# Mixture layers: routing ahead of the shared expert, routers and down projections on strips

## The chip, the cores and the metric

One core of a Trainium2 chip. The metric is the time on the device of one launch, in microseconds. PE is TensorE, DVE VectorE, ACT ScalarE, POOL GpSimd, SP SyncE, which here only issues DMAs. Each engine works through its own list of instructions in order and meets the others through semaphores.

## The reference, cut to what matters

The program is two layers over x of 4096 tokens x 256, in float32. In each, x += 0.5 ffn(norm(x)), x += mixer(norm(x)), x += 0.5 ffn(norm(x)), with the same feed-forward both times. That of the first layer is a mixture of experts, and only it is changed:

```
scores = sigmoid(x @ router_w.T)                    # 32 experts
sc     = scores + e_bias
groups: 8 of 4 experts, score = sum of the two best; keep the 3 best groups
topk   = 4 best experts by sc in those; weight = its score, normalised, * 2.5
slots  : each expert takes the first 160 tokens that chose it
Y      = (silu(X Wg) * (X Wu)) Wd for the 160 tokens of each expert
out[token] += weight * Y ;  out += (silu(x Sg^T) * (x Su^T)) Sd^T    # shared expert
```

## The kernel before, in words

`moe()` (lines 476 to 1300) is called twice; its tiles are named ffn0a (layer a below, about 0 to 247 us) and ffn0b (layer b, about 509 to 744 us). Everything is written out by hand: each engine's list of work is a sequence of helper calls, at the end of that engine's function, and that sequence is the order of execution. No planner has a part in it.

*Norm phase.* The 4096 tokens are 8 blocks of 4 tiles of 128. For a block, DVE takes the moments (`moments`), POOL works out the reciprocal deviation and the shift (lines 718 to 728), ACT applies them (`apply`, line 977, four instructions), SP stores the rows to HBM for later gathering (`rows`), PE turns the eight 128x128 pieces (`turn`, L775) into one PSUM tile `ps_a`, and ACT copies them out (`turned`, L991), so that the next turn can begin. PE then makes the router's scores (`router`, L785): a turned tile of 128 tokens is stationary, the 32-column router weight moves, k innermost, 8 matmuls a block. After four blocks ACT makes the sigmoid of one half of the tokens (`scores`, Exp, Ln, Exp). PE's list starts with a few matmuls on constants (`warm`, L177).

*Shared expert.* For each of 6 of the blocks (two more come at the end of the layer), PE does two up projections `up(n, m)` (L809), ACT the silu `gate` (L996), DVE the product `hidden` (L1119), PE the two halves of the down projection (`down`, L819) into the one tile `ps_c`, ACT copies each half out (`keep`, L1013), and SP stores it. The up projections begin in the norm phase, between the turns and routers.

*Routing.* For each half DVE scores the groups, chooses groups and experts (`score_groups` L1125, `choose_groups`, `choose_experts` L1155), and weighs the scores (`weigh`). PE counts choices by triangular matmuls (`count`, L792 to L799); DVE splits the slot numbers, then for each of 4 groups of 8 experts makes planes for the slot numbering that PE does by matmuls (`number_slots`, L397), and from it the list of tokens (`dve_tokens`).

*Experts.* POOL gathers the rows of a group's tokens by indirect DMAs, ten a group (L436); group 2 waits until all up projections are done, since it uses their room. PE turns the rows (`turn_rows`, `spread`), does the expert's two projections (`expert_up`, L866) and its down projection (`expert_down`, L888), whose results land in pieces of 128 slots: 160 slots an expert, so five pieces to four experts. In `expert_down` a piece is put together from the parts that `rows_of` gives, of 32, 64 or 128 slots, each by one matmul. ACT weighs each piece while it copies it out (`keep_y`, L1038), POOL adds it to the sums in HBM by an indirect DMA (`add`, L737), 40 of them. The gathers of the last group stand between adds 6 to 15. Then the two late blocks' sums are loaded and the next layer's head norm follows.

Of the kernel before, what the change touches and what calls it, by code (L numbers as in the profile page):

```python
# [11 lines left out]
ALU = mybir.AluOpType  # L12
# [464 lines left out]
def moe(nc, name, x, con, w, table, sums, gathered, added, turn_no, spare, combine, head, arriving=None,  # L477
# [3 lines left out]
    with Scope(nc, name) as sc:  # L481
# [9 lines left out]
        ps_r = ps_d.rearrange("p (t e) -> p t e", e=E)  # L491
# [28 lines left out]
        esg, eh = sg[:, :, 0:CAP], h[:, 0, :, 0:CAP]  # L520
# [29 lines left out]
        shift_ready = sc.sem("shift_ready")  # L550
        raw_made = sc.sem("raw_made")
        exp_made = sc.sem("exp_made")
        plus_made = sc.sem("plus_made")
# [39 lines left out]

        def finished(e):

            return (CAP * (e + 1)) // P
# [21 lines left out]
        with nc.Block() as block:  # L618
            @block.sync
            def _(sp):  # L620
# [8 lines left out]
                def rows(b):  # L629
                    sp.wait_ge(ln.xn_ready, b + 1)  # L630
                    sp.dma_start(by_tile[:, b * BT:(b + 1) * BT, 0:D], ln.xn[:, b]).then_inc(ln.xn_stored[b % 2], 16)
# [15 lines left out]
                for dst, key in zip((wg, wu, wd), ("shared_gateT", "shared_upT", "shared_downT")):  # L647
                    sp.dma_start(dst[:], w[key].rearrange("(k p) n -> p k n", p=P)).then_inc(shared_landed, 16)
# [3 lines left out]
                rows(0)  # L652
                rows(1)
                start_sums(0)
                start_sums(1)
                rows(2)
                start_sums(2)
                rows(3)
                start_sums(3)
                if not ahead:  # L660
                    sp.wait_ge(zero_set, 1)
                    clear(sp, cleared[0], range(4), zero, zero_stored)
                rows(4)
                start_sums(4)
                rows(5)
                start_sums(5)
                if arriving:
                    arriving[4]()
                rows(6)
                start_sums(6)  # L670
                shared(0)
                rows(7)
                start_sums(7)
# [7 lines left out]
                shared(1)  # L681
                if not ahead:
                    clear(sp, cleared[1], range(4), zero, zero_stored)
                weights(0)
                weights(1)
                shared(2)
                if not ahead:
                    clear(sp, cleared[1], range(4, NB), zero, zero_stored)
                    clear(sp, other, LATE, zero, zero_stored)
                    sp.wait_ge(x_stored[1], 16 * (NB - 2))  # L690
                shared(3)
                if not ahead:
                    load(0)
                    load(1)
                for n in range(4, NF):
                    shared(n)
# [14 lines left out]
            def _(pool):  # L711
# [6 lines left out]
                for b in range(NB):  # L718
# [6 lines left out]
                    after(pool, ln.xn_ready, b - 1)  # L725
# [15 lines left out]

                pool.wait_ge(ln.transposed, NB)
# [24 lines left out]
            def _(pe):  # L767
                mm = nc.tensor.matmul

                def turn(b):  # L770
                    pe.wait_ge(ln.xn_ready, b + 1)
# [7 lines left out]
                def router(b):  # L779
                    r, part = divmod(b, RT // BT)  # L780
                    pe.wait_ge(ln.xT_ready, b + 1)
                    after(pe, exp_made, r)
                    for t in range(BT):
                        for k in range(KD):
                            ins = mm(ps_r[:, part * BT + t, :], xT_of(b)[:, k, t * P:(t + 1) * P], wr[:, k, :],  # L785
                                     start=k == 0, stop=k == KD - 1)
                    ins.then_inc(raw_made, 1)

# [82 lines left out]
                def rows_of(e):  # L871

                    at, end, parts = CAP * e, CAP * (e + 1), []
                    while at < end:
                        row = at % P
                        most = {0: P, QR: QR, 2 * QR: 2 * QR, 3 * QR: QR}[row]
                        n = min(most, end - at)
                        parts.append((at // P, row, at - CAP * e, n))
                        at += n
                    open_ended = [y for y in parts if y[0] >= finished(e)]  # L880
                    return open_ended + [y for y in parts if y[0] < finished(e)]

                def expert_down(e):
                    p, r, n = e % 2, e // LW % 2, e % LW
                    pe.wait_ge(eh_made, e + 1)
                    for piece, row, at, m in rows_of(e):
                        after(pe, piece_kept, piece - 1)
                        ins = mm(ps_b[row:row + m, 2 + piece % 2, 0:D], eh[:, p, at:at + m], we[:, r, n, 2, :],  # L888
                                 start=True, stop=True)
                        if row + m == P:  # L890
                            ins.then_inc(piece_made, 1)
# [9 lines left out]
                pe.wait_ge(shared_landed, 48)  # L901
                up(0, 0)
                turn(2)
                router(1)
                up(0, 1)
                turn(3)
                router(2)
                up(1, 0)
                router(3)
                turn(4)  # L910
                up(1, 1)
                turn(5)
                router(4)
                pe.wait_ge(halved, 1)
                down(0, 0)
                turn(6)
                router(5)
                down(0, 1)
# [3 lines left out]
                up(2, 0)  # L922
                pe.wait_ge(constants_set, 1)
                count(0)
                up(2, 1)
                down(1, 0)
                down(1, 1)
                up(3, 0)
                count(1)
                down(2, 0)  # L930
                up(3, 1)
                down(2, 1)
                up(4, 0)
                number_slots(0)
                down(3, 0)
                up(4, 1)
# [1923 lines left out]
```

## Time and profile before

| | |
|---|---|
| time, median of 3 runs | 1126.53 us (1124.96 to 1128.38) |
| profiled execution | 1118.18 us, span 1116.3 us |
| busy, share of the span | PE 980.2 us (88%), DVE 723.6 (65%), ACT 549.5 (49%), POOL 379.3 (34%) |

Busy time is that of instructions, without their waits; a share is an average over stages. A row of the timeline gives the start, the duration of a run of like instructions, engine, line, operation, output and inputs, the shape, how many; in brackets how long the engine was idle before it, and what ended that. Matmuls overlap their neighbours, so the distance from one start to the next says more than a duration. The granted clock is 1.00 at 2.4 GHz and 0.50 at 1.2 GHz.

### The profile page before, as it was taken

The page shows a single profiled execution, that of the slowest core. Times are in us where ns is not written, and L with a number is a line of the kernel's source. Part 1 is how long each engine was busy: PE and PEld are TensorE (multiplying, and loading weights), DVE is VectorE, ACT ScalarE, POOL GpSimd, SP SyncE. Part 2 cuts the span into 40 slices and gives each one's busy share as a digit, 9 for nine tenths or more (in the row PEclk, how much of TensorE's full clock was granted, in tenths as well). Part 3 has the DMA queues.
Part 4 walks back from the last instruction along what each step waited for, and adds up shares of the span by engine and source line. Part 5 has one row for each costly group of instructions (what it writes and reads, how often), then busy time and mean ns, then how long its engine had stood idle before and what let it go on. Part 6 is the DMA issues. An engine that isn't in the chain of part 4 may idle for free. (4 is left out here: it accounts for less than half of the span.)

```text
span 1116.3 us, 17327 instructions
## 1 busy us (share of the span) xinstructions
PE 980.2 (88%) x5222; PEld 601.4 (54%) x5240; DVE 723.6 (65%) x2533; ACT 549.5 (49%) x1066; POOL 379.3 (34%) x452
## 2 busy tenths in 40 slices
PE   6999799979999899998999898946778799995886
PEld 4756566645565466665756665533334456552343
DVE  4588333147885476766598433158888799974886
ACT  6621233325665654547622333226657655544784
POOL 3106768810000232323006787711111256531110
PEclk9999799989999699999999999976889999996998
DMA  9859888854440902004245878766420000000012
GB/s 323 323 179 318 157 220 212 155 166 151 151 151 0 344 6 94 38 38 144 95 150 130 183 195 193 142 193 208 151 75 1 1 0 1 1 0 1 20 56 76
DMA packets 79656, 140.73 MB, mean 126 GB/s; under 512 B 16304, under 2 KB 47392, under 8 KB 77472
## 3 DMA queue, kind: packets, MB, share of 16 engines
q1 hardware_dynamic: 64224, 117.57, 30.6%
q0 software_dynamic: 15360, 22.29, 13.0%
q8 instruction: 33, 0.54, 0.2%
q14 instruction: 39, 0.32, 0.1%
HBM read 82.17 MB, written 58.72 MB: 126 GB/s over the span
## 5 line engine op out<-in xcount | busy, mean ns | idle before, releaser
L737 POOL DMA_INDIRECT ffn_sums<-ffn0a_xT,ffn0a_into x40 | 62.6, 1566 | 19.5 <-issue 8.5
L737 POOL DMA_INDIRECT ffn_sums<-ffn0b_xT,ffn0b_into x40 | 62.5, 1563 | 14.5 <-issue 9.5
L2717 PE MATMUL main_ps_k<-mixing_first_xk,mixing_wk 128*128 128x512 f32 (+1 forms) x96 | 46.7, 610 | 4.2 <-POOL main_opened_mark L1962 4.2
L1768 POOL TENSOR_TENSOR attn_attend_state_m<-attn_attend_state,attn_attend_heads 128x512 f32<-128x512 f32 x15 | 19.1, 1273 | 87.1 <-DVE attn_attend_state L1811 81.6
L1193 DVE TENSOR_TENSOR ffn0a_h<-ffn0a_sg,ffn0a_ps_b 128x160 f32<-128x160 f32 x32 | 10.3, 321 | 55.4 <-ACT ffn0a_sg L1028 55.3
L1193 DVE TENSOR_TENSOR ffn0b_h<-ffn0b_sg,ffn0b_ps_b 128x160 f32<-128x160 f32 x32 | 10.3, 321 | 53.8 <-ACT ffn0b_sg L1028 53.7
L2722 PE MATMUL attn_ps_r<-mixing_first_xr,mixing_wr 128*128 128x512 f32 (+1 forms) x96 | 45.1, 592 | 0.0
L2732 PE MATMUL attn_ps_y<-mixing_wv,attn_out 128*128 128x256 f32 (+1 forms) x192 | 43.0, 379 | 1.2 <-ACT attn_yn L2674 1.2
L866 PE MATMUL ffn0a_ps_b<-ffn0a_early,main_x 128*128 128x160 f32 x256 | 43.2, 314 | 0.7 <-DMA main_x<-w_experts 0.7
L888 PE MATMUL ffn0a_ps_b<-main_x,ffn0a_h 128*32 128x256 f32 (+2 forms) x144 | 43.5, 403 | 0.0
L888 PE MATMUL ffn0b_ps_b<-main_x,ffn0b_h 128*32 128x256 f32 (+2 forms) x144 | 43.5, 403 | 0.0
L2291 PE MATMUL main_ps_k<-dense_first_xb,main_w 128*128 128x512 bf16 x112 | 39.2, 423 | 4.7 <-issue 1.9
L1790 DVE COPY_PREDICATED main_spare<-attn_attend_causal,attn_attend_ps_a 128x1024 f32<-128x1024 int32 x32 | 40.0, 1302 | 4.5 <-issue 2.9
L866 PE MATMUL ffn0b_ps_b<-ffn0b_early,main_x 128*128 128x160 f32 x256 | 41.3, 305 | 1.5 <-DMA main_x<-w_experts 1.2
L866 PEld LDWEIGHTS ffn0a_ps_b<-ffn0a_early,main_x 128*128 128x128 f32 x256 | 38.4, 198 | 6.2 <-issue 3.8
L2732 PEld LDWEIGHTS attn_ps_y<-mixing_wv,attn_out 128*128 128x128 f32 (+1 forms) x192 | 36.3, 190 | 9.5 <-issue 3.4
L866 PEld LDWEIGHTS ffn0b_ps_b<-ffn0b_early,main_x 128*128 128x128 f32 x256 | 36.6, 190 | 7.1 <-issue 3.5
L1351 DVE TENSOR_TENSOR main_spare<-main_spare 128x1024 f32<-128x1024 f32 x28 | 34.1, 1219 | 6.8 <-POOL main_opened_mark L1962 5.9
L2593 DVE TENSOR_TENSOR_SCAN attn_st<-mixing_keep,mixing_first_carry,attn_kr 128x512 f32<-128x512 f32 (+1 forms) x24 | 31.8, 1326 | 8.6 <-ACT attn_kr L2667 8.6
L256 POOL TENSOR_TENSOR attn_head_ln_ve<-attn_head_ln_moments,attn_head_ln_eps 128x4 f32<-128x4 f32 x8 | 2.1, 266 | 103.5 <-DVE attn_head_ln_moments L232 103.5
L1811 DVE SCALAR_TENSOR_TENSOR attn_attend_state<-attn_attend_state,attn_decay,attn_attend_ps_s 128x256 f32<-128x256 f32 x32 | 14.0, 477 | 33.2 <-PE attn_attend_ps_s L1909 33.2
L1924 PE MATMUL attn_attend_ps_w<-attn_attend_wo,attn_attend_cent 128*128 128x256 f32 x128 | 31.9, 394 | 2.1 <-DVE attn_attend_cent L1805 2.1
(498 smaller groups left out, 2665.1 us busy)
## 6 DMA issues: line engine op xcount, KB each, us to landing
main_spare<-ffn_sums SPq DMA_DIRECT2D x28, 1024.0 KB, 5.5
main_x<-w_experts SPq DMA_DIRECT2D x16, 1536.0 KB, 7.0
ffn_sums<-main_lent SPq DMA_DIRECT2D x36, 512.0 KB, 6.1
ffn_sums<-main_x SPq DMA_DIRECT2D x28, 512.0 KB, 3.8
ffn_rows<-ffn0a_early SPq DMA_DIRECT2D x8, 512.0 KB, 9.3
main_spare<-ffn_sums SPq DMA_DIRECT2D x8, 512.0 KB, 4.7
ffn_rows<-ffn0b_early SPq DMA_DIRECT2D x8, 512.0 KB, 2.9
x_out<-main_x SPq DMA_DIRECT2D x8, 512.0 KB, 2.9
```

Source lines behind the costliest of these rows:

```text
L737: g.indirect_dma_start(out=sums[:, :], out_offset=IndirectOffsetOnAxis(ap=into[:, at, j:j + 1], axis=0), in_=ys[:, n % NY, :], in_offset=N ...
L866: ins = mm(ps_b[:, p, j * CAP:(j + 1) * CAP], we[:, r, n, j, k * F:(k + 1) * F], xgT[:, k, e // ME % 2, e % ME].rearrange("p a b -> p (a b)"),
L888: ins = mm(ps_b[row:row + m, 2 + piece % 2, 0:D], eh[:, p, at:at + m], we[:, r, n, 2, :], start=True, stop=True)
L1193: v.tensor_tensor(eh[:, p, :], esg[:, p, :], ps_b[:, p, CAP:2 * CAP], ALU.mult).then_inc(eh_made, 1)
L1351: v.tensor_tensor(parts[:, half, 0:2], parts[:, half, 0:2], parts[:, half, 2:4], ALU.add)\
L1790: vec.copy_predicated(att[:, p, s].rearrange("p (r n) i -> p r n i", n=2), causal[:].unsqueeze(1).unsqueeze(1).to_broadcast([P, 4, 2, P]), ...
L1924: ins = mm(ps_w[:, s, :], cent[:, 1 - p, k, s, :], wo[:, k, :], start=k == 0, stop=k == KD - 1)
L2291: ins = mm(ps[:], wt[:, k, m * P:(m + 1) * P], xb[:, p, k, :], start=k == 0, stop=k == KD - 1)
L2593: v.tensor_tensor_scan(st[0:rows, m % 2], keep[0:rows, m:m + 1].to_broadcast([rows, BN]), kr[0:rows, m % 2], carry[0:rows, p, m:m + 1], AL ...
L2717: ins = mm(ps_k[0:rows, m % 2], wk[:, k, at:at + rows], xk[:, p, k, :], start=k == 0, stop=k == KD - 1)
L2722: ins = mm(ps_r[0:rows, m % 2], wr[:, k, at:at + rows], xr[:, p, k, :], start=k == 0, stop=k == KD - 1)
L2732: ins = mm(ps_y[:, t, :], out[0:rows, p, m, t * P:(t + 1) * P], wv[0:rows, m, :], start=m == 0, stop=m == NMH - 1)
```

## The change

1. Norm. `apply` of the even blocks goes to DVE, of the odd ones stays on ACT; a semaphore for each, and `normed(b)` names the one to wait for.
2. Router. The router weight is stationary (128x32), the turned tile moves (128 columns), and the four tiles of a block go to the four 32-partition strips of a PSUM bank. The sigmoid runs on these turned scores; PE turns four 128x128 pieces back (`turn_back`) and ACT copies them out (`keep_scores`).
3. Order. On PE all turns and routers come ahead of the first up projection; on ACT the applies, copies and sigmoids ahead of the first gate; on DVE the choice of the first half ahead of the first hidden. SP loads the shared weights after x, stores the router's weights and (layer a) loads the first expert weights ahead of the first shared block.
4. `weigh` goes from DVE to POOL.
5. `expert_down` does a piece when its last expert is there: one matmul of 128 slots where the piece is all of one expert, else four strips of 32. The hidden tile of an expert has three buffers instead of two.

```diff
+        ps_raw = (ps_d, ps_c)
+        esg = sg[:, :, 0:CAP]
+        eh = [h[:, at, m, 0:CAP] for at, m in ((0, 0), (0, 1), (1, 0))]
+        def normed(b):
+            return (xn_by_act if b % 2 else xn_by_dve), b // 2 + 1
...
 # SP
-                for dst, key in zip((wg, wu, wd), ...): sp.dma_start(...)     # now after the loads of x
...
+                for b in range(NB):
+                    rows(b)
+                    start_sums(b)
...
+                weights(0)
+                weights(1)
+                if not ahead:
+                    sp.wait_ge(x_stored[1], 16 * (NB - 2))
+                    load(0)
+                    load(1)
+                shared(0)
...
 # POOL
+                def weigh(r):
+                    pool.wait_ge(score_made, r + 1)
+                    pool.wait_ge(taken_ready, r + 1)
+                    g.tensor_tensor(score[:, r], taken[:, r * RT:(r + 1) * RT, :], score[:, r], ALU.mult)\
+                        .then_inc(weight_ready, 1)
+                for r in range(NR):
+                    weigh(r)
                 pool.wait_ge(ln.transposed, NB)
...
 # PE
-                    after(pe, exp_made, r)
-                    for t in range(BT):
-                        for k in range(KD):
-                            ins = mm(ps_r[:, part * BT + t, :], xT_of(b)[:, k, t * P:(t + 1) * P], wr[:, k, :],
+                    for k in range(KD):
+                        for t in range(BT):
+                            ins = mm(ps_raw[r][t * E:(t + 1) * E, part * P:(part + 1) * P], wr[:, k, :],
+                                     xT_of(b)[:, k, t * P:(t + 1) * P], start=k == 0, stop=k == KD - 1,
+                def turn_back(r):
+                    pe.wait_ge(sigmoid_made, r + 1)
+                    for part in range(BT):
+                        ins = nc.tensor.transpose(ps_b[:, 2 + r, part * P:(part + 1) * P],
+                                                  sg[:, r, part * P:(part + 1) * P], con[:, C_IDENT:C_IDENT + P])
+                    ins.then_inc(back_made, 1)
+                def parts_of(n):
+                    parts = []
+                    for q in range(P // QR):
+                        at = P * n + QR * q
+                        parts.append((at // CAP, QR * q, at % CAP, QR))
+                    if parts[0][0] == parts[-1][0]:
+                        return [(parts[0][0], 0, parts[0][2], P)]
+                    return parts
                 def expert_down(e):
                     pe.wait_ge(eh_made, e + 1)
+                    for n in range(finished(e - 1) if e else 0, finished(e)):
+                        after(pe, piece_kept, n - 1)
+                        for of, row, at, m in parts_of(n):
+                            ins = mm(ps_b[row:row + m, 2 + n % 2, 0:D], eh[of % 3][:, at:at + m],
+                                     we[:, of // LW % 2, of % LW, 2, :], start=True, stop=True, ...)
+                        ins.then_inc(piece_made, 1)
...
 # PE's list: turn(0) turn(1) router(0) turn(2) router(1) turn(3) router(2) router(3) turn(4) turn(5) router(4)
+                turn_back(0)
 #            turn(6) router(5) turn(7) router(6) router(7)
+                up(0, 0)
+                turn_back(1)
+                pe.wait_ge(score_made, NR)
+                up(0, 1)
+                count(0)
+                up(1, 0)
+                down(0, 0)
+                down(0, 1)
+                count(1)
+                for n in range(1, NF):
+                    up(n, 1)
+                    if n + 1 < NF:
+                        up(n + 1, 0)
+                    down(n, 0)
+                    down(n, 1)
+                    if n < 4:
+                        number_slots(n - 1)
                 number_slots(3)
...
 # ACT
+                def sigmoids(r): Exp, Ln, Exp on sg[:, r] from ps_raw[r]
+                def keep_scores(r): Copy of ps_b[:, 2 + r] to score[:, r]
 # ACT's list: apply(1) turned(0) turned(1) apply(3) turned(2) turned(3) apply(5) sigmoids(0) turned(4) keep_scores(0)
 #             turned(5) apply(7) turned(6) turned(7) sigmoids(1) (wd halved) keep_scores(1) gate(0, 0) gate(0, 1)
+                for n in range(NF):
+                    if n:
+                        gate(n, 1)
+                    if n + 1 < NF:
+                        gate(n + 1, 0)
+                    keep(n, 0)
+                    keep(n, 1)
...
 # DVE
+                def apply(b): four tensor_scalar (x - mean) * rstd
-                    after(dve, piece_made, finished(e - 2) if e > 1 else 0)
+                    after(dve, piece_made, -(-CAP * (e - 2) // P) if e > 2 else 0)
+                moments(0)
+                for b in range(1, NB):
+                    moments(b)
+                    if b % 2:
+                        apply(b - 1)
 # DVE's list goes on: score_groups(0) choose_groups(0) choose_experts(0) hidden(0, 0) score_groups(1) hidden(0, 1)
 #   choose_groups(1) count_first_half choose_experts(1) with hidden(1, 0) inside, split_slots(0) hidden(1, 1)
 #   split_slots(1) planes(0, row) hidden(2, 0) planes(0, halves) planes(1, row) tokens(0) hidden(2, 1) ...
```

## Rows read from the trace of the kernel before

**Rows 1.** Grouped lines of POOL, whole span (busy us, mean ns; idle before, by releaser).

```profile
L737 POOL DMA_INDIRECT ffn_sums<-ffn0a_xT,ffn0a_into x40 | 62.6, 1566 | 19.5 <-issue 8.5 <-ACT ffn0a_xT L1038 6.9 <-DMA ffn_sums<-ffn0a_xT,ffn0a_into 4.1
...
L737 POOL DMA_INDIRECT ffn_sums<-ffn0b_xT,ffn0b_into x40 | 62.5, 1563 | 14.5 <-issue 9.5 <-DMA ffn_sums<-ffn0b_xT,ffn0b_into 3.8 <-ACT ffn0b_xT L1038 1.2
...
L436 POOL DMA_INDIRECT ffn0b_xT<-ffn_rows,ffn0b_token x20 | 20.8, 1040 | 6.1 <-issue 4.6 <-ACT ffn0b_xT L1038 1.5
```

**Rows 2.** Timeline of layer b, anchors (start us, us).

```profile
558.70 0.69 DVE L1125 TENSOR_TENSOR ffn0b_masked<-ffn0b_score,ffn0b_bias 128x512 f32<-128x512 f32 x1 [4.27 <-ACT ffn0b_score L987]
...
574.44 0.43 DVE L1155 TENSOR_SCALAR ffn0b_taken<-ffn0b_marked 128x512 bf16<-128x512 f32 x1
...
611.23 1.97 PE L819 MATMUL ffn0b_ps_c<-ffn0b_shared_down,ffn0b_h 128*128 128x256 f32 x8 [0.78 <-ACT main_x L1013]
...
614.57 1.31 PE L397 MATMUL ffn0b_ps_d<-ffn0b_val_a,main_spare 128*128 128x80 f16 x32 [1.38 <-DVE ffn0b_val_a L389]
...
615.71 1.07 PE L839 MATMUL ffn0b_ps_a<-main_con,ffn0b_early 128*128 128x128 f32 x8
...
620.27 1.90 PE L866 MATMUL ffn0b_ps_b<-ffn0b_early,main_x 128*128 128x160 f32 x12 [0.34 <-ACT ffn0b_early L1021]
...
632.86 1.62 POOL L737 DMA_INDIRECT ffn_sums<-ffn0b_xT,ffn0b_into  x1 [0.30 <-issue]
```

**Rows 3.** Timeline of PE in layer b, its pieces from start to start.

```profile
515.16 1.09 PE L775 MATMUL ffn0b_ps_a<-main_con,ffn0b_early 128*128 128x128 f32 x8 [0.72 <-ACT ffn0b_early L977]
...
526.82 1.96 PE L809 MATMUL ffn0b_ps_b<-ffn0b_xT,ffn0b_shared_gate 128*128 128x512 f32 x4
...
530.34 1.04 PE L775 MATMUL ffn0b_ps_a<-main_con,ffn0b_early 128*128 128x128 f32 x8
...
574.92 0.39 PE L792 MATMUL ffn0b_ps_a<-ffn0b_taken,ffn0b_before 128*128 128x512 bf16 x1
...
577.01 1.97 PE L819 MATMUL ffn0b_ps_c<-ffn0b_shared_down,ffn0b_h 128*128 128x256 f32 x8
...
578.82 1.02 PE L809 MATMUL ffn0b_ps_b<-ffn0b_xT,ffn0b_shared_gate 128*128 128x512 f32 x2
```

**Rows 4.** Timeline of PE in the last layer, matmuls on 32-column strips.

```profile
747.74 1.08 PE L2025 MATMUL main_ps_k<-dense_ln_xT,main_router 128*32 128x128 f32 x16 [1.17 <-ACT dense_ln_xT L2000]
...
1067.08 0.64 PE L2025 MATMUL main_ps_k<-dense_ln_xT,main_router 128*32 128x128 f32 x16
...
1067.65 0.38 PE L2300 MATMUL ffn1b_ps_c<-ffn1b_gate_t,main_pick 16*128 16x512 bf16 x1
```

**Rows 5.** Grouped lines of ACT (500 to 620 us) and of POOL (whole span).

```profile
L977 ACT ACTIVATE ffn0b_early<-main_x,ffn0b_shift,ffn0b_ln_rstd 128x256 f32<-128x256 f32 x32 | 16.3, 591 | 2.7 <-POOL ffn0b_shift L728 2.7
...
L991 ACT ACTIVATE ffn0b_xT<-ffn0b_ps_a 128x1024 f32<-128x1024 f32 x6 | 6.1, 1014 | 0.6 <-PE ffn0b_ps_a L775 0.5
...
L996 ACT ACT_TABLE_LOAD x3 | 3.8, 1283 | 0.1
...
L1768 POOL TENSOR_TENSOR attn_attend_state_m<-attn_attend_state,attn_attend_heads 128x512 f32<-128x512 f32 x15 | 19.1, 1273 | 87.1 <-DVE attn_attend_state L1811 81.6 <-PE attn_attend_ps_a L1886 5.5
```

**Rows 6.** Windows of PE: length, busy (instructions), granted clock, DMA share, GB/s.

```profile
53.00:55.00 2.00, 2.00 (x16) 0.80 1.04 384
...
55.00:57.00 2.00, 2.00 (x4) 0.50 1.02 401
...
746.00:748.00 2.00, 0.83 (x11) 0.50 0.13 18
```

**Rows 7.** Timeline of PE in layer a, down matmuls four experts apart.

```profile
199.77 1.25 PE L888 MATMUL ffn0a_ps_b<-main_x,ffn0a_h 128*32 128x256 f32 x4
...
209.57 0.40 PE L888 MATMUL ffn0a_ps_b<-main_x,ffn0a_h 128*32 128x256 f32 x1
```

**Rows 8.** Timeline of layer a, its first turn and its first add.

```profile
12.94 1.09 PE L775 MATMUL ffn0a_ps_a<-main_con,ffn0a_early 128*128 128x128 f32 x8 [1.74 <-ACT ffn0a_early L977]
...
132.46 1.62 POOL L737 DMA_INDIRECT ffn_sums<-ffn0a_xT,ffn0a_into  x1 [0.95 <-ACT ffn0a_xT L1038]
```

More of the change, by code:

```diff
@@ L651, in _ @@
                         arriving[2](n)
[L652 to L673, printed above, removed]
+                for dst, key in zip((wg, wu, wd), ("shared_gateT", "shared_upT", "shared_downT")):
+                    sp.dma_start(dst[:], w[key].rearrange("(k p) n -> p k n", p=P)).then_inc(shared_landed, 16)
+                for b in range(NB):
+                    rows(b)
+                    start_sums(b)
+                    if b == 3 and not ahead:
+                        sp.wait_ge(zero_set, 1)
+                        clear(sp, cleared[0], range(4), zero, zero_stored)
+                    if b == 5 and arriving:
+                        arriving[4]()
                 if ahead:
@@ L689, in _ @@
                     clear(sp, other, LATE, zero, zero_stored)
[L690 to L695, printed above, removed]
+                for n in range(2, NF):
                     shared(n)
@@ L1139, in mark_best @@
                     link(ins)
+                    if between:
+                        hidden(*between)
                     link(v.memset(top[:, :, n:8], LOW_MARK))
@@ L1242, in _ @@
                 choose_groups(0)
-                hidden(1, 1)
-                choose_experts(0)
-                score_groups(1)
-                hidden(2, 0)
-                choose_groups(1)
-                hidden(2, 1)
-                count_first_half()
-                choose_experts(1)
-                split_slots(0)
-                weigh(0)
-                hidden(3, 0)
+                choose_experts(0)
+                hidden(0, 0)
+                score_groups(1)
+                hidden(0, 1)
+                choose_groups(1)
+                count_first_half()
+                choose_experts(1, between=(1, 0))
+                split_slots(0)
+                hidden(1, 1)
                 split_slots(1)
@@ L1256, in _ @@
                 index.dve_planes(0, row)
-                weigh(1)
+                hidden(2, 0)
                 index.dve_planes(0, tile_a)
-                hidden(3, 1)
                 index.dve_planes(0, tile_b)
```

165 lines of the change are left out of this document (53 added, 112 removed).

## The prediction

> **What bounds the kernel now.** I read the busy shares first: PE is busy most of the span, POOL a third of it; those are averages, and the change touches only the two mixture layers (called a and b here, about 0 to 247 and 509 to 744 us). Next the grouped lines of POOL: in each layer the 40 scatter-adds stand 62.5 us busy beside 14.5 (b) and 19.5 (a) of idle, of which 9.5 and 8.5 are POOL's own issue: an add at POOL's own pace is 1.56 and up to 0.3, 1.86 [rows 1]. With the ten gathers of the last group between them ((20.8 + 6.1) / 20 = 1.34 each) they fill the end of the layer: POOL is the bound there, and little of its idle is another engine's doing (b: DMA 3.8, ACT 1.2; a: ACT 6.9, DMA 4.1). So a layer's length is the start of its first add plus that loop. The timeline says what sets this start. In b PE ends its shared expert at 611.23 plus 1.1, the last slot numbering starts at 614.57, the first expert matmul at 620.27 and the first add at 632.86 [rows 2]. Two lines race to that add: PE's in-order list up to the first expert, and POOL's gathers of group 2, which wait for the shared expert's last up projection, because they reuse its buffers, and then take 10 x 1.34 = 13 us.
>
> **The change, part by part.** It takes the shared expert's work out of the gaps of the norm phase and puts it behind the routers; so the question is whether the norm phase gets shorter by as much as PE's later list gets longer.
>
> *Norm phase.* Per pair of blocks ACT has one apply (16.3 / 8 = 2.04) and two copies of turned blocks (1.01 each) [rows 5]; the other apply goes to DVE, which has slack. The turned tile has one buffer, so the second turn waits for the first copy and the second copy for that turn: 1.09 at full clock [rows 3] and 0.1 of hops. A pair takes 2.04 + 1.01 + 1.2 + 1.01 = 5.25, four take 21. The three sigmoid passes and the copy-back over 128x512 are half-size against 1.01: 2.0, with hops 2.5; the last routers trail by 1.4. From the first turn, 515.16 [rows 3], the last router ends at 515.2 + 21 + 2.5 + 1.4 = 540.1. The strip routers cost little: 16 strip matmuls of the same shape take 0.57 from start to start at full clock, and a row of 1.08 in a stage at half [rows 4].
>
> *Clock.* This is where I choose. PE keeps 2.4 GHz through the present norm phase because projections fill its gaps. Where the present kernel leaves turns and old routers by themselves, the granted clock falls to 0.80 and then 0.50 within 4 us, and the next projection's first four matmuls, at full clock 1.8, don't end within that window of 2 us [rows 6]. In a later stage turns and strip routers with gaps stay at 0.50 [rows 6]. After the change PE does only these, and about half the time, for some 25 us. I take it to fall to 1.2 GHz. Then a turn is 2.0 instead of 1.1 (a pair 6.15, four 24.6) and the last routers trail by 2.2: the last router ends at 544.5.
>
> The Trainium skill, "TensorE: Matmul & The Clock Gate", Part 4, says that transposes do not count as busy for the gate as matmuls do; by that rule the clock falls here as in rows 6, and the sum is the one with 1.2 GHz. The trace agrees (0.80, 0.50).
>
> *From the last router to the second half's choice.* One projection (526.82 to 530.34 = 3.5; at half clock about 1.5 more) [rows 3], the turn back 0.5, the copy 0.6, ACT's table load 1.28 [rows 5], the gate 0.6, and DVE's hidden 0.7 stand one behind another, since the new order puts hidden(0,0) ahead of the second half's scoring: 540.1 + 7.2 = 547.3, at half clock 544.5 + 8.7 = 553.2. Then DVE does score_groups, two hiddens, choose_groups, the first half's count and choose_experts, as it does now between 558.70 and 574.44 + 0.43: 16.2 [rows 2]. The choice is there at 563.5 (569.4), where it is 574.9 now: 11 (5.5) earlier, and the first token list and POOL's first gathers with it.
>
> *PE behind it.* count(1) waits for this choice, and PE's order is fixed. Three projections and two downs lie ahead of it, 10.5 + 3.6 and the first count 2.1 and the turn back 0.5, in a stretch of 563.5 - 540.1 = 23.4: PE idles some 6 us, which would be another reason for the clock to fall. Behind it stand count(1) 2.1, nine projections x 3.5 = 31.6, ten downs x 1.81 = 18.1 [rows 3], four slot numberings x 1.14 (614.57 to 615.7) = 4.6 [rows 2]: 56.4. Each second down of a block waits for ACT's copy of the first: five times 0.78 [rows 2] = 3.9. Where a hidden stands behind index work on DVE (a row of planes and two halves), PE waits too: I allow 3.7, between nothing and five times the 1.38 that the last slot numbering waits now [rows 2]. Sum 64.0: the last numbering ends at 627.5 (633.4). From there to the first expert now 4.56 (615.71 to 620.27): 632.1 (638.0), against 620.27. The first add follows by one expert's up, gate, hidden, one piece and its copy, 4.6 as I estimate it (1.3 for eight up matmuls at the pace of the first twelve, 1.90 [rows 2], 0.6 for the gate, 0.4 for hidden, 1.1 for two pieces, 0.6 for the copy, hops 0.6), with 2 to either side; today's 12.6 can't be its size, since the gathers set it. So the first add moves from 632.86 to 636.7 (642.6): 3.8 or 9.7 later. Now it is the gathers that hold it 12.6 behind the first expert; then the gathers, behind a last projection that ends at 627.5 - 1.1 - 3.6 - 0.8 = 622, are through by 622 + 0.5 + 13.4 = 636 and tie with PE.
>
> *Layer a.* The same order, from the first turn at 12.94 [rows 8] by the same distance, 632.1 - 515.2 = 116.9: first expert at 129.8 (135.8), add at 134.4 (140.4), against 132.46: 1.9 or 7.9 later.
>
> *Expert loop.* Four experts take PE 199.77 to 209.57 = 9.80 [rows 7]; the ups at the pace above take 4 x 1.27, so nine down matmuls take 4.7, 0.53 each. New: three sets of four strips and two full matmuls. If strips overlap as in rows 4, a set of 256 columns is twice 0.57 / 2 = 0.57, so 3 x 0.57 + 2 x 0.53 = 2.8: PE gains 1.9 per four experts, 15 a layer. POOL needs 5 x 1.86 + 1.25 x 1.34 = 11.0 for the same pieces, so this stays hidden; only waits on ACT's copies can shrink. I take 4 of the 6.9 in layer a, 0 in b; the ends are 0 and 6.9 + 1.2. No row shows strips of 256 columns with a changing weight, so the cost of a set lies between 0.57 and 4 x 0.53 = 2.1.
>
> The Trainium skill, "TensorEngine Tiling (Array Packing)", Key Properties, says that a change of the tiling mode drains TensorE; this speaks against a loop that goes from strips to full matmuls with every expert. By it a set would cost more than 0.57; rows 4 show no such drain (the next instruction of another shape starts 0.57 after 16 strips).
>
> *The rest.* weigh goes to POOL: 1.27 each by the nearest row of that shape [rows 5], twice, while POOL has nothing but norm steps and waits for tokens some 15 us away; if it were late, 2.5. SP's queue gets the shared weights later and the expert weights earlier; the first user of either stands behind the last router. Two table loads fewer on ACT (1.28 each) lie in the norm phase of which I have already counted what is left. Those I set at 0 with ends of -2.5 and +2.5.
>
> **Sum.** With the clock low: b +9.7, a +7.9 - 4 = +3.9: +13.6. The profiled execution (1118.2) then gives 1131.8; it lies 8.3 below the median 1126.53, to which I add the same: 1140.
>
> **The rivals.**
> A, the clock stays high in the norm phase. For it: the four filling matmuls between the first turns remain. Against it rows 6. Then +3.8 + 1.9 - 4 = +1.7: 1128, no change.
> B, faster: PE does not wait for the second choice, and its list sets the first expert. Without that idle and the waits of 3.7 and 3.9: 540.1 + 12 x 3.5 + 12 x 1.81 + 2 x 2.1 + 4.6 + 0.5 = 613.1, first expert 617.7; the last projection ends 4.8 before 613.1 and the gathers 13.9 later, so the add comes at about 622, 10.6 earlier in b, and by the same distance at 120 in a, 12.5 earlier and 4 more in the loop. Half of the 27 gives 1113, all of it 1100. It decides if the choice comes before 540.1 + 16.7 = 557. For it: DVE loses its 4.27 wait for the second score in the old place. Against it: 16.2 of chained DVE work behind the first hidden is in the order itself.
> C, slower: strips one behind another. Then 14 x 0.53 = 7.4 instead of 4.7 per four experts, PE at 12.5 against POOL's 11.0: 1.5 x 8 x 2 = +24, on the forecast 1164. It decides from a set of about 1.6 us. Against it rows 4.
> D, the norm phase isn't shortened because something else paces it (in a the arrival of the blocks): another +3 to +5, inside the forecast's own range.
>
> **How the numbers follow.** Forecast (D included) 0.5; A 0.2; B 0.23; C 0.07. Forecast's own range 1132 to 1150, from the allowance of 3.7 (0 to 6.9 in each layer), the 4.6 (by 2), and the 4 (0 to 8). The range of 8 in 10 reaches through A to the weaker half of B: 1112 to 1150. About 0.3% (3.4 us, so 1123 to 1130) is what a measurement of this kernel can tell from no change. Faster: B and a little of A, 0.27. Same: most of A and the forecast's lower edge, 0.17. Slower: 0.56.
>
> **What would show it.** Granted clock near 0.50 between the second turn and the first projection; the second choice near 569 and first expert near 638 counted from a start of 509 in b; an idle stretch of PE before its second count; the add loop no shorter than now in b; PE's matmuls per four experts near 7.9 us. The prediction is wrong if the first add comes before 632.86 counted from the same start, or if the adds begin to run faster than 1.86 apart.

## The result, and the profile after

1141.59 us (1137.32 to 1144.88) against 1126.10 (1124.96 to 1128.38): a ratio of 1.0142, interval 1.0119 to 1.0166, so 13 to 19 us slower. 1140 was forecast. The page of the changed kernel shows how the work shrank while the time grew: PE has 20 us less to do than before, in a span 23 us longer (the profiled execution of before lies 8 us below its median, that of the changed kernel at its own; of the 23, 6.5 lie in layer a up to its last add, 11.8 in layer b, 1.6 between the two and 3.6 behind them, where nothing was changed). Every distance below is from one profiled execution of a kernel, and such an execution can lie several us from the median of its kernel.

```profile
span 1139.7 us, 17686 instructions
PE 960.4 (84%) x5416; PEld 581.8 (51%) x5416; DVE 732.1 (64%) x2561; ACT 526.4 (46%) x1030; POOL 388.2 (34%) x456
```

The timeline of layer b, which now starts 8.0 us later (first turn 523.17, in place of 515.16 [rows 3]), PE and DVE in the order of time, then POOL; the bracket is the engine's idle time before the row:

```profile
523.17 1.04 PE L779 MATMUL ffn0b_ps_a<-main_con,ffn0b_early 128*128 128x128 f32 x8
...
537.82 1.94 PE L779 MATMUL ffn0b_ps_a<-main_con,ffn0b_early 128*128 128x128 f32 x8 [3.10 <-ACT ffn0b_xT L995]
...
542.58 0.69 DVE L1125 TENSOR_TENSOR ffn0b_masked<-ffn0b_score,ffn0b_bias 128x512 f32<-128x512 f32 x1 [6.72 <-ACT ffn0b_score L990]
...
549.53 1.98 PE L820 MATMUL ffn0b_ps_b<-ffn0b_xT,ffn0b_shared_gate 128*128 128x512 f32 x4
...
572.44 0.61 PE L803 MATMUL ffn0b_ps_a<-ffn0b_taken,ffn0b_before 128*128 128x512 bf16 x1 [4.54 <-DVE ffn0b_taken L1156]
...
573.27 3.41 PE L810 MATMUL ffn0b_ps_a<-ffn0b_taken,ffn0b_ones 128*128 128x480 bf16 x15
...
590.74 1.84 PE L397 MATMUL ffn0b_ps_d<-ffn0b_val_a,main_spare 128*128 128x80 f16 x32 [2.09 <-DVE ffn0b_val_a L389]
592.38 3.11 PE L820 MATMUL ffn0b_ps_b<-ffn0b_xT,ffn0b_shared_gate 128*128 128x512 f32 x4
...
639.64 1.31 PE L397 MATMUL ffn0b_ps_d<-ffn0b_val_a,main_spare 128*128 128x80 f16 x32
...
645.30 2.44 PE L877 MATMUL ffn0b_ps_b<-ffn0b_early,main_x 128*128 128x160 f32 x16 [0.34 <-ACT ffn0b_early L1025]
...
634.44 1.00 POOL L436 DMA_INDIRECT ffn0b_xT<-ffn_rows,ffn0b_token  x1 [11.93 <-PE ffn0b_ps_b L820]
...
650.72 1.62 POOL L732 DMA_INDIRECT ffn_sums<-ffn0b_xT,ffn0b_into  x1 [3.55 <-ACT ffn0b_xT L1042]
```

Read it as a relay. The last router is done at 549.5, 26.4 after the first turn; that part is shorter than before. PE then waits 4.54 us for the second choice, comes out of the wait at half clock (15 matmuls of the count take 3.41, in place of 1.80 in the kernel before, whose row stands below), and works down its list to 640.8. POOL, which had its first gathers early, stands idle 11.93 us until the last projection has freed the room for group 2, and 3.55 more until ACT hands it the first piece. Before, the gathers ran without a break into the first add; now PE's list leads and POOL waits. From first turn to first add layer b takes 650.72 - 523.17 = 127.55 us, where it took 632.86 - 515.16 = 117.70 [rows 2, 3]: 9.85 more. Layer a: 142.00 - 12.89 = 129.1 against 119.5 [rows 8]: 9.6 more. The count in the kernel before, and the first add of layer a after:

```profile
575.36 1.80 PE L799 MATMUL ffn0b_ps_a<-ffn0b_taken,ffn0b_ones 128*128 128x480 bf16 x15
```

```profile
142.00 1.63 POOL L732 DMA_INDIRECT ffn_sums<-ffn0a_xT,ffn0a_into  x1 [3.56 <-ACT ffn0a_xT L1042]
```

The windows of PE (length, busy, granted clock, DMA share, GB/s) say when the clock falls:

```profile
526.00:530.00 4.00, 3.02 (x48) 1.00 0.61 207
530.00:534.00 4.00, 2.59 (x43) 1.00 0.83 295
534.00:538.00 4.00, 0.90 (x8) 0.83 0.83 280
538.00:542.00 4.00, 3.81 (x28) 0.50 0.27 87
570.00:574.00 4.00, 1.56 (x4) 0.60 0.00 0
574.00:578.00 4.00, 4.00 (x16) 0.55 0.76 197
586.00:590.00 4.00, 1.97 (x8) 1.00 0.00 0
590.00:594.00 4.00, 3.26 (x34) 0.66 0.32 131
```

Three falls in this execution, each at a wait: for the turn behind the first sigmoid (3.10 us), for the second choice (4.54), and for the first slot numbering, where DVE's planes come late (2.09; a wait of 0.78 for ACT stands shortly before). Through the 8 us of turns and strip routers before 534, which follow the constant matmuls of `warm`, with waits up to 1.2 us, the clock stayed at 1.00. That the same waits do not always end in a fall is shown by e4_old_down below.

The loop of adds, as POOL's grouped lines show it (to be set beside [rows 1]):

```profile
L732 POOL DMA_INDIRECT ffn_sums<-ffn0b_xT,ffn0b_into x40 | 62.5, 1563 | 19.7 <-issue 10.4 <-ACT ffn0b_xT L1042 5.2 <-DMA ffn_sums<-ffn0b_xT,ffn0b_into 4.1
L732 POOL DMA_INDIRECT ffn_sums<-ffn0a_xT,ffn0a_into x40 | 62.5, 1563 | 19.1 <-issue 9.2 <-ACT ffn0a_xT L1042 6.5 <-DMA ffn_sums<-ffn0a_xT,ffn0a_into 3.3
```

Of ACT's 5.2 (b) and 6.5 (a), 3.55 stand ahead of the first add, outside the loop. From first to last add: a 90.4 us (93.5 before), b 91.0 (89.0). So PE's quicker down projection is hardly seen here, though the grouped lines of PE in layer b show it plainly: 224 instructions in 27.1 us, where 144 took 43.5. What PE gains it waits for, in part, on the experts' weights (7.7 us in four waits; 1.2 before). The new order of SP's loads is not the reason: e3 and e6 below, which have the new down projection and the old order of loads, wait 8.6 and 9.5 us for them.

```profile
L898 PE MATMUL ffn0b_ps_b<-main_x,ffn0b_h 128*32 128x256 f32 (+1 forms) x224 | 27.1, 416 | 0.6 <-DVE ffn0b_h L1188 0.6
```

```profile
L888 PE MATMUL ffn0b_ps_b<-main_x,ffn0b_h 128*32 128x256 f32 (+2 forms) x144 | 43.5, 403 | 0.0
```

```profile
PE ffn0b_ps_b L877 <- DMA main_x<-w_experts: 7.7, 4, 3.9
```

And a set of four strips of 256 columns, in layer a's timeline, takes 0.57 from start to start; to the set four experts on (four experts, with one piece of index work in between) it is 7.96:

```profile
199.99 0.64 PE L898 MATMUL ffn0a_ps_b<-main_x,ffn0a_h 128*32 128x256 f32 x8
200.56 0.67 PE L863 MATMUL ffn0a_ps_c<-ffn0a_by_piece,main_con 128*128 128x80 f32 x4
...
207.95 0.64 PE L898 MATMUL ffn0a_ps_b<-main_x,ffn0a_h 128*32 128x256 f32 x8
```

### The profile page after: what moved, and what is told of

It reads as the page before. It is cut to its first block and busy times, and to the rows that moved or that the text cites. A ratio compares the mean times of both kernels' runs of the same rounds, so it can differ in the third digit from the quotient of the medians.

```text
span 1139.7 us, 17686 instructions
## 1 busy us (share of the span) xinstructions
PE 960.4 (84%) x5416; PEld 581.8 (51%) x5416; DVE 732.1 (64%) x2561; ACT 526.4 (46%) x1030; POOL 388.2 (34%) x456
## 5 line engine op out<-in xcount | busy, mean ns | idle before, releaser
L2284 PE MATMUL main_ps_k<-dense_first_xb,main_w 128*128 128x512 bf16 x128 | 45.1, 438 | 0.5
L830 PE MATMUL ffn0b_ps_c<-ffn0b_shared_down,ffn0b_h 128*128 128x256 f32 x112 | 28.6, 401 | 10.3 <-DVE ffn0b_h L1119 5.6
L830 PE MATMUL ffn0a_ps_c<-ffn0a_shared_down,ffn0a_h 128*128 128x256 f32 x112 | 28.3, 397 | 8.6 <-ACT main_x L1017 4.7
L1000 ACT ACTIVATE ffn0a_sg<-ffn0a_ps_b 128x512 f32<-128x512 f32 x14 | 8.4, 597 | 54.8 <-PE ffn0a_ps_b L820 54.8
```

The lines of the kernel that those rows point to most:

```text
L830: ins = mm(ps[:, i, :], h[:, n % 2, m, t * P:(t + 1) * P], wd[:, m, :], start=m == 0, stop=m == 1)
L2284: ins = mm(ps[:], wt[:, k, m * P:(m + 1) * P], xb[:, p, k, :], start=k == 0, stop=k == KD - 1)
```

## The experiments

The theory: the first expert comes late because PE's fixed list puts nine projections behind a count that waits for the second choice, with the clock down on top; POOL covers the rest. The rivals: the clock alone; one of the new parts; DVE's index work or the gathers. All times of the table but the last column's are counted from the layer's first turn, from one profiled execution each; a / b are the layers. The second count is given by its second matmul, which starts 0.2 us (at half clock 0.4) behind the end of the wait for the choice. Some profiled executions lie far from their kernel's median: before 8 us below, e7_both 8 below, e4_old_down 5 below, e3_strips_only 6 above. So differences of 2 or 3 us in this table are within its spread; the ratios are from all fast runs.

| kernel | ratio to before (95%) | last router starts | second count | first expert | first add | adds, first to last |
|---|---|---|---|---|---|---|
| before | 1 | 39.9 / 39.3 | 60.6 / 60.0 | 112.6 / 105.1 | 119.5 / 117.7 | 93.5 / 89.0 |
| changed | 1.0142 (1.0119 to 1.0166) | 27.3 / 25.8 | 51.0 / 49.7 | 123.7 / 122.1 | 129.1 / 127.6 | 90.4 / 91.0 |
| e1_clock | 1.0077 (1.0046 to 1.0108) | 25.0 / 25.0 | 49.1 / 49.1 | 117.5 / 117.5 | 123.0 / 123.0 | 93.3 / 92.6 |
| e2_up11 | 1.0080 (1.0027 to 1.0132) | 27.3 / 25.8 | 50.9 / 49.5 | 119.6 / 114.2 | 125.0 / 119.6 | 92.0 / 92.4 |
| e7_both | 1.0076 (1.0043 to 1.0108) | 25.0 / 25.0 | 49.1 / 49.1 | 118.7 / 113.7 | 124.2 / 119.1 | 89.7 / 91.2 |
| e4_old_down | 1.0197 (1.0155 to 1.0239) | 27.4 / 25.0 | 51.1 / 49.4 | 121.0 / 119.1 | 126.5 / 124.5 | 93.6 / 93.2 |
| e3_strips_only | 0.9976 (0.9953 to 1.0000) | 39.9 / 39.3 | 62.3 / 60.0 | 115.5 / 104.9 | 121.8 / 118.2 | 93.6 / 90.4 |
| e9_half_norm | 1.0003 (0.9974 to 1.0032) | 40.3 / 40.3 | 62.6 / 61.0 | 115.1 / 105.9 | 121.7 / 117.9 | 93.8 / 89.3 |
| e13_strip_router | 0.9985 (0.9961 to 1.0010) | 41.0 / 36.9 | 62.2 / 57.9 | 111.9 / 104.6 | 121.4 / 115.9 | 95.1 / 88.3 |
| e6_old_order | 0.9940 (0.9911 to 0.9970) | 36.0 / 36.0 | 57.2 / 57.0 | 108.2 / 102.0 | 115.4 / 114.1 | 95.0 / 90.5 |
| e10_earlier_scores | 0.9920 (0.9888 to 0.9952) | 35.0 / 35.0 | 58.0 / 57.0 | 110.1 / 101.9 | 116.8 / 113.9 | 91.7 / 88.3 |

**e1_clock: the clock held up.** Constant matmuls in PE's three waits.

```diff
                 turn(4)
+                warm(nc, con, ps_b[:, 0], 3)
                 turn(5)
                 router(4)
                 turn_back(0)
+                warm(nc, con, ps_b[:, 0], 1)
...
                 down(0, 1)
+                warm(nc, con, ps_d[:], 4)
                 count(1)
...
+                    if n == 1:
+                        warm(nc, con, ps_d[:], 2)
                     if n < 4:
                         number_slots(n - 1)
```

> The changed kernel with constant matmuls put into the three stretches in which PE waits (four of them in the norm phase before the sixth and seventh turn, four ahead of the second count, two ahead of the first slot numbering); order and all other work as changed. If the low clock carries most of the loss (the forecast against its rival A): granted clock 1.00 from the first turn to the first expert, last router, second choice and first expert 3 to 5 us earlier after the first turn, first add 6 to 8 us earlier in each layer, 1127 to 1131 us. If the order alone carries it: under 3 us off 1141.6.

The time fell from 1141.59 to 1133.55 (the ratio to before from 1.0142 to 1.0077), between the two expectations. The windows of that run that answer to those above (first turn at 517.68):

```profile
525.00:529.00 4.00, 2.23 (x44) 1.00 0.63 216
529.00:533.00 4.00, 4.00 (x30) 1.00 0.83 284
533.00:537.00 4.00, 3.25 (x31) 1.00 0.49 162
564.00:568.00 4.00, 2.50 (x12) 1.00 0.00 0
```

Its timeline behind the second choice shows the count back at 1.80, and the first expert:

```profile
566.54 0.39 PE L803 MATMUL ffn0b_ps_a<-ffn0b_taken,ffn0b_before 128*128 128x512 bf16 x1 [1.50 <-DVE ffn0b_taken L1161]
...
566.98 1.80 PE L810 MATMUL ffn0b_ps_a<-ffn0b_taken,ffn0b_ones 128*128 128x480 bf16 x15
...
635.22 2.03 PE L877 MATMUL ffn0b_ps_b<-ffn0b_early,main_x 128*128 128x160 f32 x13 [0.34 <-ACT ffn0b_early L1030]
```

So the clock carries about half the loss: the first expert comes 6.1 (a) and 4.6 us (b) sooner. But the front gives little of it. The second count starts only 2.0 and 0.6 sooner, because DVE, from the first half's score on, works some 30 us without a break to the second choice (0.4 us of waits in the changed kernel's layer b, none shown here), and that first score comes only 1.8 (a) and 0.4 us (b) sooner. In b the score is 536.68 - 517.68 = 19.0 after the first turn, where it was 542.58 - 523.17 = 19.4:

```profile
536.68 0.69 DVE L1130 TENSOR_TENSOR ffn0b_masked<-ffn0b_score,ffn0b_bias 128x512 f32<-128x512 f32 x1 [4.66 <-ACT ffn0b_score L995]
```

The rest, 4.1 and 4.0, lies behind the count. Both layers end their adds less far ahead of the changed kernel (3.2 and 3.0), since the loop got 2.9 and 1.6 longer.

**e2_up11: one projection ahead of the count.**

```diff
                 down(0, 1)
+                up(1, 1)
                 count(1)
                 for n in range(1, NF):
-                    up(n, 1)
+                    if n > 1:
+                        up(n, 1)
```

> The changed kernel with one projection, up(1,1), moved from behind the second count to ahead of it, into PE's idle stretch of 4.5 us. If PE's list behind the second count sets the first expert (forecast): the count isn't later, the list behind it is 3.5 shorter and its clock stays up (2.5), first add 5 to 6 us earlier in each layer, 1129 to 1132 us. If DVE's index work or POOL's gathers set the first add instead: no gain, 1139 to 1143.

1132.67, just above the 1129 to 1132 expected: the first add comes 4.1 (a) and 8.0 us (b) sooner, 6 a layer as expected in the mean. PE's list behind the second count is what sets it; POOL's gathers and DVE's index work allowed all of it in b. Only 3.5 of the 8.0 are the projection itself. PE's wait for the second choice shrank to 1.12 us, the count behind it took 1.80 again, and the first slot numbering 1.31, so most of the rest is clock, and the run does not separate the two. In a PE waited 3.42 us, in place of 0.78, for a copy of ACT that waited for a store (see e7):

```profile
113.19 0.60 ACT L1019 ACTIVATE main_x<-ffn0a_ps_c 128x512 f32<-128x512 f32 x1 [3.77 <-DMA ffn_sums<-main_x]
```

That this gain and that of e1 can't be added is shown by the next run.

**e7_both:** the matmuls of e1 in the norm phase and ahead of the first slot numbering, and the projection of e2 in the place of those ahead of the count.

> The changed kernel with constant matmuls in the norm phase and ahead of the first slot numbering, and up(1,1) moved ahead of the second count. The clock (8 us of the loss by the first run) and the idle stretch (9 by the second) share the slow second count, so the two don't add up: first add 3 us earlier than with the constant matmuls alone, 1126 to 1130 us. If they were independent: 1122 to 1125.

1130.43, a ratio of 1.0076, no better than either; what makes up the rest of the loss was not found, and the profiled execution can't tell, since it is the fastest of six (1122.09). In b the first add is 3.8 us sooner than in e1, as expected; in a it is 1.2 later. There something else ends last. ACT's copy of a shared block waits for the store of an earlier one, and PE's down projection behind it:

```profile
112.26 0.60 ACT L1023 ACTIVATE main_x<-ffn0a_ps_c 128x512 f32<-128x512 f32 x1 [4.46 <-DMA ffn_sums<-main_x]
```

```profile
113.00 3.65 PE L830 MATMUL ffn0a_ps_c<-ffn0a_shared_down,ffn0a_h 128*128 128x256 f32 x8 [4.11 <-ACT main_x L1023]
```

The DMA engines are 0.98 to 1.04 busy from 70 to 110 us in that layer, which alone has the clearing of the sums in its queue. So in a, as I read it, the shared expert, pushed together behind the routers, runs into the stores; no run moved the clearing away to show it.

**e3_strips_only** and **e4_old_down: the new down projection given and taken away.** e3 is the kernel before with the new `expert_down`, `parts_of` and three hidden buffers; e4 the changed kernel with the old ones:

```diff
-        esg = sg[:, :, 0:CAP]
-        eh = [h[:, at, m, 0:CAP] for at, m in ((0, 0), (0, 1), (1, 0))]
+        esg, eh = sg[:, :, 0:CAP], h[:, 0, :, 0:CAP]
...
-                        for of, row, at, m in parts_of(n):
...
+                    for piece, row, at, m in rows_of(e):
...
```

> The kernel before with the new down projection of the experts alone (strips, three hidden buffers). If POOL bounds the expert loop: PE's matmuls for four experts fall from 9.8 to about 7.7 us and the time stays, 1121 to 1127 us, the add loop at most 4 us shorter in layer a. If the loop is PE's: 10 us or more faster. If strips cost more than their overlap gives: slower.

> The changed kernel with the old down projection of the experts (two hidden buffers, parts of 32, 64 and 128 slots). If POOL bounds the loop: first add unchanged, 1141 to 1147 us, the most of it in layer a's adds. If the new down projection has part in the loss: faster than 1139.

e3: 1122.70, 0 to 5 us faster by its interval, although PE does the same experts in 16 us less per layer. e4: 1143.64. Its interval overlaps with that of the changed kernel, and its loop of adds is 2 to 3 us longer. Both say the same: POOL hides nearly all of it, and it has no part in the loss.

One thing in e4 was not expected: its first add comes 2.6 (a) and 3.1 us (b) sooner, though up to the first expert its work and order are those of the changed kernel. The clock did it. In b PE waits the same 3.10 us behind the first sigmoid and 2.10 ahead of the first slot numbering, and the clock stays at 1.00 behind both; in a it stays up behind the second of them:

```profile
536.28 1.06 PE L778 MATMUL ffn0b_ps_a<-main_con,ffn0b_early 128*128 128x128 f32 x8 [3.10 <-ACT ffn0b_xT L996]
...
586.45 1.31 PE L397 MATMUL ffn0b_ps_d<-ffn0b_val_a,main_spare 128*128 128x80 f16 x32 [2.10 <-DVE ffn0b_val_a L389]
```

```profile
535.00:539.00 4.00, 2.23 (x28) 1.00 0.63 212
586.00:590.00 4.00, 3.55 (x38) 1.00 0.30 119
```

So with the same list a wait of that length can end in a fall or not. It is also a second measure of the clock: without the fall at the first slot numbering, and with a shorter one at the count, the first expert comes 2.6 (a) and 3.0 us (b) sooner.

**e9_half_norm** and **e13_strip_router: two more parts alone,** in the order of before: four of the eight applies on DVE; the strip router with the sigmoid on turned scores, in one PSUM bank and turned back into it.

```diff
-                apply(0)
                 apply(1)
                 turned(0)
-                apply(2)
...
+                moments(0)
+                for b in range(1, 6):
+                    moments(b)
+                    if b % 2:
+                        apply(b - 1)
```

```diff
+                    for k in range(KD):
+                        for t in range(BT):
+                            ins = mm(ps_d[t * E:(t + 1) * E, part * P:(part + 1) * P], wr[:, k, :], ...)
...
                 turn(5)
+                turn_back(0)
                 router(4)
...
                 up(2, 0)
+                turn_back(1)
```

> The kernel before with half of the norms applied on DVE, in the order of before otherwise. If ACT paced the norm phase: second count 1 to 4 us earlier after the first turn, and 0 to 5 us faster, 1120 to 1126. If DVE or PE did: same as before, or up to 3 us slower, since the applies delay DVE's first hiddens.

> The kernel before with the strip router and the sigmoid on turned scores alone (one PSUM bank, turned back into the same bank). If the shorter router is what makes the version with the old order faster (second count 3.4 us earlier there): second count 57 to 59 after the first turn, first add 1 to 4 us earlier, 1117 to 1124 us. If it needs the half norms beside it (ACT paces): as before, 1122 to 1128.

Neither moves the time by more than its interval (1.0003, 0.9985). With the router alone the second count comes 2.1 us sooner in b, and 1.6 later in a; but e3, whose front is that of before, has it 1.7 later in a too, so in a that much is spread. With half of the norms alone it comes 2.0 (a) and 1.0 us (b) later. Together, in e6, they bring it 3.4 and 3.0 sooner.

**e6_old_order: all parts, the old order.** The two diffs above and the new down projection together in the kernel before, projections in the norm phase as they were; `weigh` stays on DVE.

> All parts of the change but the order: the kernel before, with its interleaving of projections into the norm phase, with half of the norms on DVE, strip routers with the sigmoid on turned scores (in one PSUM bank, turned back into the same bank), and the new down projection; weigh stays on DVE. If the order is what costs, and the parts are free or better: second count at 54 to 59 after the first turn (60 now), first add 3 to 8 us earlier than before in each layer, 1108 to 1122 us. If one of the parts costs: at or above 1126.

1117.79, 0.994 (0.9911 to 0.9970): faster than before, and 2% faster than the changed kernel, which differs from it by the order (SP's too), by `weigh`, and by the banks that the router writes. No run moves these apart, but `weigh` can be ruled out by the changed kernel's trace: POOL does the second one in 1.16 us, right behind the choice, and then has nothing to do for 21.41 us until its first gather:

```profile
572.53 1.16 POOL L741 TENSOR_TENSOR ffn0b_score<-ffn0b_taken,ffn0b_score 128x512 f32<-128x512 bf16 x1 [15.38 <-DVE ffn0b_taken L1156]
...
595.10 1.13 POOL L436 DMA_INDIRECT ffn0b_early<-ffn_rows,ffn0b_token  x1 [21.41 <-DVE ffn0b_token L421]
```

The rows of e6's layer b (first turn at 511.62) show POOL going from the last gather into the first add with its own 0.30 only, while PE had its first expert 12 us ahead of that add:

```profile
613.62 1.08 PE L884 MATMUL ffn0b_ps_b<-ffn0b_early,main_x 128*128 128x160 f32 x6 [0.34 <-ACT ffn0b_early L1045]
```

```profile
624.37 1.00 POOL L436 DMA_INDIRECT ffn0b_xT<-ffn_rows,ffn0b_token  x1 [0.30 <-issue]
625.67 1.62 POOL L747 DMA_INDIRECT ffn_sums<-ffn0b_xT,ffn0b_into  x1 [0.30 <-issue]
```

**e10_earlier_scores: the same with the scores drawn forward** (PE's part of the edit; ACT's sigmoid and DVE's scoring of the first half move ahead likewise).

```diff
                 router(2)
-                up(1, 0)
                 router(3)
                 turn(4)
-                up(1, 1)
+                up(1, 0)
+                turn_back(0)
                 turn(5)
-                turn_back(0)
                 router(4)
+                up(1, 1)
...
-                up(2, 0)
                 turn_back(1)
+                up(2, 0)
```

> The version with the old order and all parts, with the scores drawn forward: the fourth router ahead of up(1,0), the first half's sigmoid ahead of gate(1,0), the second turn back ahead of up(2,0). If the choice, and through it POOL's first gather, sets the first add there (first gather 74 and first add 114 to 115 after the first turn): second count 2 to 4 us earlier, first add as much, 1110 to 1117 us. If PE's list is the bound again: no gain, 1115 to 1121.

1112.71, 0.992 (0.9888 to 0.9952), the fastest kernel here; its interval overlaps with that of e6, so it is not shown to be faster than that. The time lies in the range expected, but the mechanism expected did not show: the second count is where it was (58.0 / 57.0) and the first add is no earlier (1.4 later in a, 0.1 sooner in b). The loop of adds is 2 to 3 us shorter instead; why was not tried.

## Why the prediction was right, and where it was not

**The path.** Right in each link: the last router earlier, PE idle ahead of the second count (6 us said, 4.5 measured), the first expert later, POOL waiting for PE where before POOL's own gathers had set the first add. The sum at half clock had the first add 9.7 (b) and 7.9 us (a) later; it came 9.85 and 9.6 later. That the total came within 2 us of 1140 is in part luck. From profile to profile the two layers grew by 18.3 (first add 19.4, loops -1.1), where the sum had 13.6, and the whole by 23.4; by the medians it is 15.5. The sum went from a profiled execution that was 8 us fast to a median, and errors of some us cancel there.

**PE behind the second choice.** 64.0 us to the end of the last slot numbering was the sum; with the clock up it is 111.9 + 1.1 - 48.9 = 64.1 (e1, b, from the end of the wait), and in the changed kernel 640.8 - 572.4 = 68.4. The sum was right for 2.4 GHz, which was assumed for this stretch; its step that failed is that assumption, by 4.3 us. The second choice, which starts this stretch, came 49.3 behind the first turn, 564.4 on the old start: where the sum with the clock high had it (563.5), not the one that was chosen (569.4).

**The clock: size right by luck, place and reason wrong.** 5.9 us a layer were put on the norm phase (last router 29.3 after the first turn instead of 24.9, and a slow first projection). Measured, the last router ends at 26.4 (b) and 27.9 (a), 0.8 and 2.3 behind e1; the first projection runs at full clock (549.53, 1.98). The second count is 0.6 and 2.0 late. The other 4 us lie behind the count, in two falls that the sum did not price. The sum holds in total, 6.1 and 4.6 by e1, only because these two were left out as the first was overpriced. The reason given was that turns and strips do not keep the clock up; the windows show 8 us of them at 1.00, and the fall behind the wait of 3.1 us, and e4's layer b goes through the whole norm phase, that wait included, at 1.00. By the Trainium skill, "TensorE: Matmul & The Clock Gate", Part 4, transposes do not count as busy in the way that matmuls do; this trace has turns mixed with strip matmuls, and through these 8 us the clock did not fall.

**The first add behind the first expert.** 4.6 estimated, 5.4 measured, within its 2.

**The tie of the gathers.** 636 against 636.7 was the forecast; the gathers end 3.6 us ahead of the first piece, so PE leads clearly.

**The loop.** Layer a was to gain 4 and gained 3.1; layer b was set at 0 and lost 2.0. With the first add earlier the loops grow to 92 to 93 us in both layers in e1 and e2, but not in e7 (89.7 and 91.2). What ends last in them was not settled: POOL's waits there spread over its own issue, DMA and ACT.

**The down projection.** 0.57 a set, 7.9 for four experts, 15 us a layer off PE, hidden: measured 0.57, 7.96 and 16.4, hidden (e3, e4). Rival C, strips one behind another, falls. The Trainium skill, "TensorEngine Tiling (Array Packing)", Key Properties, has a drain at each change of mode; at 0.57 a set, with full matmuls on both sides, no run here shows a cost of it.

**Rival A** had 1128 with the clock up, 1.7 above before; e1, which holds it up, measures 1.0077, 5 to 12 us above before. The order costs more than the +1.7 of that sum: 1.5 more a layer up to the first add (123.0 where the sum has 121.5), and the loops, which did not give the 4 in a and are 3.6 longer in b than before. **Rival B** needed the choice by 41.8 after the first turn; it came at 49 to 51, since DVE does 30 us of work in one chain from the first score on. **Rival D** falls: the norm phase got shorter, the last router starting 12.6 (a) and 13.5 us (b) sooner than before.

**The order against the parts.** The prediction priced the parts near nothing and the order as the loss. e6 shows this, as far as SP's order and the router's banks, which go with the order, are not the cause: with the parts alone the kernel is 0.6% faster, with the order on top 1.4% slower. What the forecast of the whole did not say is that the parts together gain 3 to 10 us, because it counted the norm phase only as the new order has it.

## What to carry to other kernels

A list that an engine works in order can be shorter and still end later, if the work that filled its waits is moved behind the last of them; count what stands behind the last wait, not the sum. When a stage is made denser ask what stood in its gaps. Here the projections in the norm phase held the last router back (36.0 in e6, 25.8 to 27.3 in the changed kernel) but not the first add; moved behind the routers they stood ahead of the first expert, which came 11 and 17 us later than before, about 5 of these the clock's. Price a low clock at each wait of the new order, not only where the work is thin, and as a range: the same wait ended in a fall in one kernel and not in the other.

## What the hardware showed that was not expected

In the changed kernel's layer b the granted clock stayed at 1.00 through 8 us of transposes and strip matmuls with waits up to 1.2 us, and fell behind waits of 3.10, 4.54 and 2.09 us; the work behind the wait then ran at half speed until it rose again (3.41 us in place of 1.80 for the count). The length of a wait alone does not tell whether it falls. In e4, with the same list, it stayed at 1.00 behind 3.10 (b) and 2.10 us (a and b), and in the kernel before it fell to 0.50 among turns and routers with a single wait of 0.44:

```profile
554.44 2.27 PE L785 MATMUL ffn0b_ps_d<-ffn0b_wr,ffn0b_xT 128*128 128x32 f32 x16 [0.44 <-ACT ffn0b_xT L991]
```

```profile
556.00:558.00 2.00, 2.00 (x6) 0.50 0.54 215
```

What decides it was not found. The filled waits of e1 kept it at 1.00 in every window shown.
